# Mixture of experts in one kernel: all eight experts for every token, or only the two chosen, with rows sorted through DRAM

## The reference

```
x      = layernorm(t)                       # per token
probs  = softmax(x @ router.T)              # 8 values
p1, p2 = the two largest, divided by their sum
out    = t + sum over all e of gate[e] * (w2[e] @ (silu(w1[e] @ x) * (w3[e] @ x)))
```

## Time and profile before

| | us |
|---|---|
| median of three runs | 3072.85 (3072.46 to 3079.17) |
| the profiled execution's own time | 3068.73 |
| its span | 3066.9 |
| first two parts | 0 to about 2548.7 |
| staging block of the experts | 2548.7 to about 2597.7 |
| four batches of experts | 2597.7 to 3066.9 |

### The profile page before, as it was taken

How to read it: one execution, slowest core, us unless ns; L and a number is a source line. 1 busy time by engine, 2 the same in 40 slices (tenths; PEclk the granted TensorE clock), 3 DMA queues, 4 the chain that set the end, 5 groups by cost and what they waited for, 6 DMA issues and landing times. The chain is left out here.

```text
span 3066.9 us, 48595 instructions
## 1 busy us (share of the span) xinstructions
PE 2601.3 (85%) x17280; PEld 1736.8 (57%) x17280; DVE 1813.7 (59%) x3117; ACT 1364.7 (44%) x2816; POOL 635.5 (21%) x607
## 2 busy tenths in 40 slices
PE   5666577663899999899997999997999993998999
PEld 3544445343566665566664666665666652777777
DVE  4755658474466566466555556654656644766755
ACT  2323333231355554455553555553555453544544
POOL 0331405043011011011001001101101112544445
PEclk9777788776799999999998999999999995999999
DMA  2451706257755655546565565654655602000000
GB/s 88 171 195 68 293 27 267 75 216 226 151 120 126 126 105 115 131 102 137 107 130 111 107 130 117 135 117 98 135 117 121 131 3 102 4 18 7 17 11 8
DMA packets 191886, 342.32 MB, mean 112 GB/s; under 512 B 65632, under 2 KB 95040, under 8 KB 191152
## 3 DMA queue, kind: packets, MB, share of 16 engines
q1 hardware_dynamic: 191664, 339.49, 43.8%
HBM read 224.56 MB, written 112.99 MB: 110 GB/s over the span
## 5 line engine op out<-in xcount | busy, mean ns | idle before, releaser
L1342 ACT ACTIVATE prob<-ps 128x512 f32<-128x512 f32 (+5 forms) x1600 | 636.8, 441 | 740.0 <-PE ps L1293 586.1
L1395 DVE TENSOR_REDUCE maxima<-ps 128x1 f32<-128x512 f32 (+3 forms) x768 | 387.4, 547 | 297.6 <-PE ps L1224 149.6
L1314 PE MATMUL ps<-prob,plain 128*32 128x512 f32 (+5 forms) x3200 | 512.0, 443 | 0.0
L1365 POOL TENSOR_TENSOR products<-products,sums 128x256 f32<-128x256 f32 x192 | 140.6, 732 | 1609.0 <-DVE sums L1386 1607.7
L1400 DVE TENSOR_REDUCE maxima<-ps 128x2 f32<-128x512 f32 (+1 forms) x512 | 294.4, 607 | 244.1 <-PE ps L1242 108.6
L1386 DVE RECIPROCAL sums<-sums 128x256 f32<-128x256 f32 x192 | 331.5, 1736 | 104.0 <-ACT sums L1353 104.0
L1285 PE MATMUL ps<-q1a_s,k1a_s 128*128 128x512 f32 (+3 forms) x768 | 303.2, 395 | 0.0
L1293 PE MATMUL ps<-q1b_s,k1b_s 128*128 128x512 f32 (+3 forms) x768 | 301.1, 393 | 0.0
L1314 PE MATMUL ps<-prob,v_s 128*32 128x512 f32 (+3 forms) x1536 | 284.3, 491 | 0.0
L1670 POOL TENSOR_TENSOR hl<-hid,hh 128x512 fp32r<-128x512 f32 x176 | 229.2, 1302 | 262.2 <-ACT hh L1614 257.8
L1221 PE MATMUL ps<-k1a_s,q1a_s 128*128 128x512 f32 (+3 forms) x768 | 234.6, 374 | 5.9 <-DMA k1a_s<-k1ah_dram 5.9
(11 more groups left out here) (300 smaller groups left out, 5623.2 us busy)
## 6 DMA issues: line engine op xcount, KB each, us to landing
qh_dram<-pairs SPq DMA_DIRECT2D x96, 512.0 KB, 3.7
kwh_dram<-pairs SPq DMA_DIRECT2D x64, 512.0 KB, 2.7
qa_s<-qh_dram SPq DMA_DIRECT2D x128, 256.0 KB, 4.3
kwa_s<-kwh_dram SPq DMA_DIRECT2D x128, 256.0 KB, 7.4
q1a_s<-qh_dram SPq DMA_DIRECT2D x128, 256.0 KB, 4.7
qb_s<-qh_dram SPq DMA_DIRECT2D x64, 256.0 KB, 9.1
kwb_s<-kwh_dram SPq DMA_DIRECT2D x64, 256.0 KB, 10.1
k1a_s<-k1ah_dram SPq DMA_DIRECT2D x32, 512.0 KB, 6.7
```

The lines of the kernel that those rows point to most:

```text
L1314: mm = pe.matmul(ps[at:at + VD, SCORES + k % 2, q0 - c * CH:q0 - c * CH + w], w_, m.prob[:, n % PROBS, h, 0:w], start=first, stop=True, sk ...
L1342: act.activation(m.prob[:, u % PROBS, h, 0:w], ps[:, turn % SCORES, 0:w], ACT.Exp, scale=SCALE).then_inc(s["exp_done"], 1)
L1365: pool.tensor_tensor(o, o, m.sums[:, br, cc], ALU.mult).then_inc(s["divided"], 1)
L1395: ins = dve.tensor_reduce(partial[:, h, i, part:part + 1], bank[:, 0:w], AX, ALU.max)
```

## The change

The experts part is rewritten as two blocks in sequence, without a loop over batches.

`route_block` prepares all 32 tiles of 128 tokens at once. It transposes, normalizes, transposes back and makes the logits. It ranks the experts as before, and in addition counts: with one matmul against a triangular matrix and one against ones it gets each token's place among the tokens of its expert within a tile and the count of each tile; five doubling steps add the counts over the tiles. Each expert gets whole tiles of 128 places; there are at most 64 + 7 = 71 of them (SLOTS), and always 71 are worked through. GpSimd then sends each token's normalized row, with its number as a 129th word, to its two places in a DRAM array `xs` of 71 x 128 rows, by 64 indirect DMAs of 128 rows. The array has been filled before with zero rows whose number is out of bounds. Each tile's expert is written to `owner`.

`experts_block` goes through the 71 tiles. A tile's rows are loaded (four tiles per DMA), transposed and split. PE reads the tile's expert into a register and uses it as an index into the weights: six matmuls with the tokens stationary and 342 units moving, three transposes, and six matmuls by w2 (three of 256 columns that hold w2's high and low halves, three of 128). GpSimd returns the 128 result rows by an indirect DMA to a second DRAM array `ys`, where rows with the number out of bounds are dropped. When all tiles are done, both results of each token are loaded back, weighted, added to t, transposed and stored.

```diff
-TILES = -(-NE * HID // P)
+TILES_OF = B * T // P
+PAIRS_OF = 2 * TILES_OF
+SLOTS = PAIRS_OF + NE - 1
+HIDP = HID + 1
...
-    with nc.Fori(0, B - 1) as b:
-        experts_block(nc, m, (t2_dram[0:B - 1][b], out[0:B - 1][b]), t2_dram[1:B][b])
-    experts_block(nc, m, (t2_dram[B - 1], out[B - 1]), None)
+    with ExitStack() as mem:
+        route_block(nc, m, d, t2_dram, lambda *a: mem.enter_context(nc.sbuf_tensor(*a)))
+    experts_block(nc, m, out, sb)
...
+def route_block(nc, m, d, t2_dram, sb):
...
+        def _(sp):
+            for b in range(B):
+                sp.dma_start(t2[:, b, :], t2_dram[b]).then_inc(s["t_loaded%d" % b], 16)
...
+            for k, name in enumerate(("w1", "w3", "w2")):
+                sp.dma_start(raw[k][:], d[name]).then_inc(s["w_loaded"], 16)
+            sp.wait_ge(s["empty_set"], 2)
+            sp.dma_start(m.xs.rearrange("(i p) n -> p i n", p=P),
+                         empty[:].unsqueeze(1).to_broadcast([P, SLOTS, ROW])).then_inc(s["cleared"], 16)
...
+        def _(pool):
...
+            for g in range(groups):
+                gg = slice(GROUP * g, GROUP * (g + 1))
+                pool.wait_ge(s["xn_done"], GROUP * (g + 1))
+                pool.tensor_copy(xe[1][:, gg, 0:P], xe[0][:, gg, 0:P]).then_inc(s["copied"], 1)
+            pool.wait_ge(s["cleared"], 16)
...
+            pool.wait_ge(s["placed"], 1)
+            for t in range(TILES_OF):
+                for k in range(2):
+                    pool.indirect_dma_start(m.xs, bass.IndirectOffsetOnAxis(ap=where[:, k, t:t + 1], axis=0),
+                                            xe[k][:, t, :], None, bounds_check=SLOTS * P - 1, oob_is_err=False)\
+                        .then_inc(s["scattered"], 16)
+            pool.wait_ge(s["scattered"], 16 * PAIRS_OF)
...
+def experts_block(nc, m, out, sb):
...
+            def hidden(i):
+                g = i // GROUP
+                e = pe.value_load(m.owner[0:1, i:i + 1], min_val=0, max_val=NE - 1)
...
+                pe.matmul(h1, x, m.w1[0][:, e, :], start=True, stop=False)
+                pe.matmul(h1, x, m.w1[1][:, e, :], start=False, stop=False)
+                pe.matmul(h3, x, m.w3[0][:, e, :], start=True, stop=False)
+                pe.matmul(h3, x, m.w3[1][:, e, :], start=False, stop=False)
+                pe.matmul(h1, xl, m.w1[0][:, e, :], start=False, stop=True).then_inc(s["h1_ready"], 1)
+                pe.matmul(h3, xl, m.w3[0][:, e, :], start=False, stop=True).then_inc(s["h3_ready"], 1)
...
+            def output(i, e):
+                pe.wait_ge(s["lo_done"], i + 1)
+                if i >= 1:
+                    pe.wait_ge(s["y_done"], i)
...
+            for i in range(SLOTS + 2):
+                if i < SLOTS:
+                    owner[i] = hidden(i)
+                if i % GROUP == 1 and i // GROUP + 1 < loads:
+                    turn_x(i // GROUP + 1)
+                if 1 <= i <= SLOTS:
+                    turn_h(i - 1)
+                if i >= 2:
+                    output(i - 2, owner[i - 2])
...
+        def _(pool):
+            for i in range(SLOTS):
+                g = i // GROUP
+                pool.wait_ge(s["y_done"], i + 1)
+                at = bass.IndirectOffsetOnAxis(ap=m.xin[:, g % 3, i % GROUP, P:ROW].bitcast(I32), axis=0)
+                pool.indirect_dma_start(m.ys, at, m.y[:, i % 4, :], None, bounds_check=2 * B * T - 1, oob_is_err=False)\
+                    .then_inc(s["put%d" % (i % 4)], 16)
...
+            for i in range(SLOTS + 2):
+                if i < SLOTS:
+                    middle(i)
+                if i % GROUP == 1 and i // GROUP + 1 < loads:
+                    lower(i // GROUP + 1)
+                if 1 <= i <= SLOTS:
+                    low(i - 1)
+                if i >= 2:
+                    result(i - 2)
```

More of the change, by code:

```diff
@@ L1492, in experts_block @@
[L1492 to L1498, removed]
-    stack = ExitStack()
[L1500 to L1520, removed]
@@ L1535, in _ @@
[L1535 to L1540, removed]
+            for b in range(B):
+                sp.dma_start(t2[:, b, :], t2_dram[b]).then_inc(s["t_loaded%d" % b], 16)
+            small = ((router, "router"), (tie, "tie"), (before, "before"), (token, "token"), (steps, "steps"),
+                     (places, "places"))
@@ L1542, in _ @@
+            sp.wait_ge(s["w_loaded"], 48)
+            sp.wait_ge(s["small_loaded"], 16 * len(small))
         @block.tensor
         def _(pe):
[L1544 to L1555, removed]
[L1556 to L1562 removed]
@@ L1650, in _ @@
-            if batch:
-                split(NC * TILES - 1)
-            if following is not None:
-                if batch:
-                    act.wait_ge(s["used"], NC * TILES)
-                act.copy(m.xh[:], m.xhn[:]).then_inc(s["moved"], 1)
+            for g in range(groups):
+                act.wait_ge(s["turned"], g + 1)
+                act.copy(m.t_tok[:, GROUP * g:GROUP * (g + 1), :], ps[:, g % 2, :].rearrange("p (t n) -> p t n", t=GROUP))\
+                    .then_inc(s["t_copied"], 1)
@@ new lines, in _ @@
+            all_ = src[:, TILES_OF - 1, :]
+            tiles, base, end, start = [count[:, k, :] for k in range(4)]
+            by_step = more[:, 0:NE, 0:TILES_OF]
+            run(dve.tensor_tensor(by_step, all_.unsqueeze(2).to_broadcast([P, NE, TILES_OF]), each_token(steps[:], NE),
+                                  ALU.is_gt))
+            run(dve.tensor_reduce(tiles, by_step, AX, ALU.add))
+            square = same[:, 0, :].rearrange("p (a b) -> p a b", a=NE)
+            run(dve.tensor_tensor(square, tiles.unsqueeze(1).to_broadcast([P, NE, NE]), tie[:], ALU.mult))
@@ new lines, in _ @@
+            run(dve.tensor_reduce(base, square, AX, ALU.add))
+            dve.tensor_scalar(start, base, float(P), None, ALU.mult)
+            run(dve.tensor_tensor(end, base, tiles, ALU.add))
+            run(dve.tensor_tensor(pos[:], three(0), start.unsqueeze(1).to_broadcast([P, TILES_OF, NE]), ALU.add))
+            run(dve.tensor_tensor(pos[:, 1:], pos[:, 1:], src[:, 0:TILES_OF - 1], ALU.add))
+            picked = [more[:, :, k * NE:(k + 1) * NE] for k in range(2)]
+            for k in range(2):
+                run(dve.tensor_tensor(picked[k], chosen[:, k], pos[:], ALU.mult))
+                run(dve.tensor_reduce(slot[:, k, :], picked[k], AX, ALU.add))
@@ new lines, in _ @@
+            dve.tensor_copy(where[:], slot[:]).then_inc(s["placed"], 1)
+            gated = [same[:, :, k * NE:(k + 1) * NE] for k in range(2)]
+            for k in range(2):
+                run(dve.tensor_tensor(gated[k], chosen[:, k], gt[:], ALU.mult))
+                run(dve.tensor_reduce(m.gate[:, k, :], gated[k], AX, ALU.add))
+            run(dve.tensor_tensor(above[:], places[:].unsqueeze(2).to_broadcast([P, SLOTS, NE]), each_token(end, SLOTS),
+                                  ALU.is_ge))
```

566 lines of the change are left out of this document (324 added, 242 removed).

## The result

The changed kernel takes 2935.90 us (median of four runs, 2932.05 to 2938.53); the kernel before, beside it, 3074.56 (3072.46 to 3079.17). The ratio is 0.9546, 95% interval 0.9529 to 0.9563: 139 us, 4.5% faster. The profiled execution took 2938.53, its span is 2936.4. The first two parts, which are unchanged, ended 2.9 us later than in the trace of before (2551.7 for 2548.78), as unchanged code does from one profile to another; so the stages are compared from the start of the part.

A forecast was written before the change was run, and what follows sets the result against it. It took the old batches to be bound by matmul columns. Routing 76, sending 90 + 4, fill 6, tiles 213 + 6 and return 36 made 431 us for 518, 87 less: 2986 us, range 2895 to 3125 (8 in 10).

The forecast's parts named there:

- rival A: Whole part: only engines count, address registers hidden, tile 2.3 us, GpSimd send 0.9; 349 us, 169 less, 2904; chance 0.25.
- places known: Routing of all 32 tiles, with nothing hiding it, until each token's place is known: 76 us into the part.
- sends, landing, border: 64 serial indirect DMAs on GpSimd at 1.4 us, 90, plus last landing 2 and block border 2.
- tiles, drain, landing: Expert tile loop: 71 tiles at 3.0 us, 213, plus drain 4 and last landing 2.
- return: Loading results back, adding, transposing and storing at the end: 36 us, of which 16 loads take 27.
- T: Time for one tile in the expert loop: 3.0 us taken, from 2.2 to 3.5.
- the ring: Tile loop: output, result, next output; high 0.71, low 0.71, result 0.58, handovers 0.24 give 2.24 us a tile.
- output waits for y_done just before six of those addresses, so half or more is exposed: Tile loop: reason for taking 3.0 us a tile, with 1.3 us of register work that may show.
- the five us for GpSimd's copies beside the normalization: Routing: eight GpSimd copies of 128x512 add 5 us, since GpSimd and DVE shut each other out.
- DVE's 64 additions hide: Return: 64 DVE additions at 0.35 us lie hidden in the loads of 27 us.
- B: GpSimd's 135 indirect DMAs bound the part; at 3.5 us each 600 us, 82 more, 3155; chance 0.17.
- C: Tile loop: address waits keep TensorE at 1.2 GHz, tile 4.5 us; part 538 us, 20 more, 3093; chance 0.13.

The follow-up runs named there:

- `early_number`: Changed kernel with each tile's expert number read into the register one tile ahead, behind the previous tile's six matmuls; 2925.16 us, ratio 0.9516.
- `static_expert`: Changed kernel with each tile's expert taken from a fixed table, so no register load or register addresses in the tile loop; 2920.17 us, ratio 0.9503.
- `best4`: `best2` with four buffers instead of three for the loaded rows; 2906.99 us, ratio 0.9456.
- `best1`: Changed kernel with `early_number` and `logits_between`, plus weights' high halves made by ACT in six pieces between its group copies; 2923.63 us, ratio 0.9512.
- `best2`: `best1` with ACT making the first copy of the result and DVE only the addition; 2910.93 us, ratio 0.9471.
- `sum_in_psum`: Changed kernel with w2's low-half product added in the accumulator: nine 128-column output matmuls, one DVE copy as result; 2942.42 us, ratio 0.9574.
- `low_first`: Changed kernel with DVE's three weight subtractions moved ahead of its wait for the logits, ACT's copies ahead of its exponential; 2933.69 us, one run.
- `logits_between`: Changed kernel with each group's logits made right after the next group is turned back, not after all groups; 2940.81 us, one run.

## Why the prediction was right, and what was mis-sized

2986 was forecast and 2935.9 measured, in the range (2895 to 3125) and in the forecast's own (2925 to 3075), between the forecast and rival A (2904). The gain was under-rated by 50 us. Of these 6.6 is the step from the profiled execution to the median: I added 4, and this kernel's profiled run is 2.6 above its median; 2.9 the other way is the start of the part. The 46.3 that remain, against the marks of the prediction:

| | forecast | measured | |
|---|---|---|---|
| places known | 76 | 66.8 | -9.2 |
| sends, landing, border | 94 | 95.6 | +1.6 |
| fill | 6 | 5.5 | -0.5 |
| tiles, drain, landing | 219 | 186.6 | -32.4 |
| return | 36 | 30.2 | -5.8 |
| the part | 431 | 384.7 | -46.3 |

- **The tiles: the term that was mis-sized.** T is 2.526 for 3.0, 71 x 0.47 = 34 us. The mechanism stands in outline: limits of about 2.2 us from TensorE, DVE and the ring, and register work on top. Its size was off: I exposed 0.8 of 1.3 us, "half or more"; removing the register gives back 0.286. The 1.3 us were themselves too many. The trace has seven operations for addresses a tile, not twelve (one of 46 ns before the first of the six matmuls and three of 32 behind it, three of 46 for the output), 0.28 us where I put 0.96; the reading is dearer (a load of 0.30 and 0.15 behind it, for which I took 0.34). And the step "output waits for y_done just before six of those addresses, so half or more is exposed" failed: there is such a wait (16.7 us in all over 71 tiles), but 12.5 us of it stay without any register, and most of what the register costs comes from the reading, which stands before the other six matmuls (0.209 of 0.286 by `early_number`).
- **The ring: right at 2.24 partly by luck.** I added 2.24 us from the end of a tile's transposes to the end of the result before it. In `static_expert` that stretch is 1.83 (the 2.32 above less 0.49 of transposes), and yet T is 2.240. What makes up the rest of that tile is not shown; `best4`'s 2.144 is near the 2.13 added up for TensorE alone.
- **Routing.** The statistics (14.4 for 16), the logits (13.66 for 14.3) and DVE's chain (26.6 for 26; 2.29 for 2.3 and 0.42 for 0.42) came as computed: the scaling by element count from the earlier trace rows holds. What failed is the five us for GpSimd's copies beside the normalization: from statistics to the last normalized row it was 11.2 where 18 stood, with 8 normalizations in 2.43 and 2.69. (1.1 of the 18 is a slip: 16 and 1 + 10.8 + 5 make 32.9, not 34. The 335 GB/s under the clear is another, 320 by its two rows; it changes its 30 us by 2.) The clear landed 39.6 us after its issue, 46.9 into the part, for 55, and was hidden as said.
- **Sending.** 1.28 us for 1.4, and 3 longer ones: 5.2 us where I gave the subtractions 9 at most. That nearly cancels, and from the last send's start to the first load it is 9.2 where 5.4 was in the sum (one send 1.4, landing and border 4).
- **Return.** Not the loads (1.7 each, 27 us) but DVE's additions bound it, 32 pairs at 0.65, 20.8 us; "DVE's 64 additions hide" is reversed, at a smaller sum. This is read from the timeline, not tested.
- **Rival A** (T 2.3, sends 0.9) was right that the array can go on at about that pace, but the changed kernel did not: T falls to 2.3 only where the register is read early or not at all, and a send costs 1.28, not 0.9. **B** is excluded by the 1.28 us and GpSimd's 126.8 us of waits. **C** by the clock of 1.00 from 2730 on; the idle 92.5 us of sending, at 0.50, cost the first tiles only the 19 us stretch at 0.70.

The Trainium skill, DMA: Bandwidth & Descriptors, section Anatomy of one DMA on the SWDGE (gpsimd) path, gives a fixed 2.0 us that is mostly completion latency. The trace agrees with the latency (landings at 2.2 to 2.3 us, mostly) and shows that it overlaps with the next send: 1.28 from send to send.

## What to carry to other kernels

A stage with a data-dependent order has to be priced by its serial part: here 3.4 times fewer matmul columns (176 x 10 x 512 = 901,000 for 71 x (6 x 342 + 3 x 256 + 7 x 128) = 264,000) made a part 1.35 times shorter (518.1 to 384.7): the tiles alone became 2.5 times shorter (469.2 to 186.6), and 198 us of routing, sending and return stand beside nothing. When an engine reads a register for each step, read it one step ahead; it gave 14 us of tiles for a moved line. "Issue" before an idle stretch is not a cause: two stretches of 16 us bore the same word here, and one went with the place of the register reading (15.5 to 1.9), the other with DVE's share of the result (17.1 to 6.5, `best1` to `best2`). An experiment that relieves one engine and loads another, as `sum_in_psum` does, has to be read by its waits and not by its time. And what holds a buffer until a result has landed belongs into the sum, as `best4` showed.

What stays open: how much of `best4`'s 2.144 is the array alone (2.13 by the prediction's sum, so little is left by it); whether the 0.077 left in `early_number` is the addresses or the moved reading; whether DVE's own time or the ring held `static_expert` at 2.240; what ACT's copy of the result alone gives in the changed kernel, with the register still read late; whether the sends could be hidden by routing batch by batch while tiles of an earlier batch run; what a second accumulator for the result would give. The last three were not tried.

## What the runs showed of the hardware that was not expected

- A row scatter of 128 rows costs GpSimd 0.98 us, the same for rows of 516 bytes from `xe` and for 512 bytes from `y_out`, and 0.30 to the next one where they follow one another; it lands in 2.2 to 2.3 us (median), with 64 or 128 in a row.
- DVE's subtraction of two on-chip arrays holds such a scatter up: those that start at 2622.65, 2625.57 and 2628.48 end 0.87, 0.86 and 0.85 us after the subtraction they overlap. The one that started at 2621.37, 0.02 us after a subtraction did, was not held. The Trainium skill, SBUF — State Buffer, section SBUF: two separate sides, describes an exclusive lock that GpSimd and certain DVE instructions, those with two on-chip inputs among them, take for a whole instruction, and a GpSimd DMA whose descriptors cannot be written while DVE holds it. The trace agrees for these three sends, which end soon after the subtraction does, and `low_first` for the cause.
- DVE's normalization with one on-chip input next to GpSimd's copies went nearly free (2.43 and 2.69 us for eight; 336 ns in the median and 637 at most), where in before one took 6147 ns beside a GpSimd instruction with two on-chip inputs.
- TensorE reads a word into a register in 0.30 us, with 0.15 of register work behind it; an operation for an address costs 32 to 46 ns, where SyncE needed 51 + 29.
- TensorE, busy for 16 us without a gap with transposes and matmuls of 8 columns, stays at a granted clock of 0.50 (`logits_between`, 2576 to 2592); in the tiles it has 1.00.
